# A transformer block in eight batches: two feed-forward moments taken between two score stages, and the tensor engine's order rewritten around them

## What is computed

```python
h = causal_conv1d(x, cond)                    # cond as taps, + bias
q, k, v = split(h @ qkv_w.T + qkv_b)          # 16 heads of 32
a = softmax(q k^T / sqrt(32) + alibi, causal) # first attention, 256 x 256 per head
x = x + (a v) @ out_w.T + out_b
Q, K, V = Wq, Wk, Wv applied along the tokens # second attention: 512 positions, 16 heads of 16
y = softmax((Q K^T / 4 + att_b) masked by cond) V
x = x + (silu(y @ gate_w.T) * (y @ up_w.T)) @ down_w.T
```

## Time and profile before

| what | value |
|---|---|
| three runs, without a profile | 1383.13, 1386.01 (median), 1388.77 us |
| profiled execution: its own time | 1393.41 us |
| profiled execution: span of the trace | 1391.6 us |
| PE busy in the span | 1223.9 us (88%) |
| DVE, ACT, POOL busy | 760.9 (55%), 522.3 (38%), 353.8 us (25%) |
| mean granted clock of PE in the span | 0.943 of full speed |
| one batch, second to seventh | 158.4 to 161.3 us |
| feed-forward of the last batch at the end | about 45 us |

### The profile page before, as it was taken

How to read it: one execution, slowest core, us unless ns; L and a number is a source line. 1 busy time by engine, 2 the same in 40 slices (tenths; PEclk the granted TensorE clock), 3 DMA queues, 4 the chain that set the end, 5 groups by cost and what they waited for, 6 DMA issues and landing times.

```text
span 1391.6 us, 21059 instructions
## 1 busy us (share of the span) xinstructions
PE 1223.9 (88%) x7528; PEld 683.2 (49%) x7528; DVE 760.9 (55%) x1173; ACT 522.3 (38%) x698; POOL 353.8 (25%) x202
## 2 busy tenths in 40 slices
PE   4485579899989999899998999889998999899988
PEld 3152235555445545546455555446455554455436
DVE  5344762557644674447724684447825585446732
ACT  1221145223533245323542246322552235332562
POOL 3075750065000920037000740027100550000000
PEclk9698579999999999999999999999999999999999
DMA  9866914255043722267042641257042650447124
GB/s 335 227 214 199 303 32 97 95 136 188 6 107 132 180 100 48 61 170 220 22 106 104 174 135 37 72 157 227 27 106 82 144 185 4 107 139 204 42 107 166
DMA packets 80481, 180.89 MB, mean 130 GB/s; under 512 B 14404, under 2 KB 54292, under 8 KB 70708
## 3 DMA queue, kind: packets, MB, share of 16 engines
q1 hardware_dynamic: 78352, 175.21, 43.2%
q0 software_dynamic: 1280, 4.20, 1.2%
q10 hardware_dynamic: 768, 0.26, 0.1%
HBM read 106.41 MB, written 21.14 MB: 92 GB/s over the span
## 4 chain that ended last, share of the span: by engine, by line
PE 66%; DVE 15%; DMA 6%; SPq 5%; issue 4%; ACT 2%; POOL 2%; DVEq 0%; ACTq 0%; POOLq 0%
PE psum L1076 9%; PE psum L1027 8%; PE psum L864 8%; PE psum L906 5%; DVE max L771 4%; PE psum L907 4%; PE psum L908 4%; PE psum L895 4%; PE psum L870 4%; SPq L392 4%; PE psum L1001 3%; PE psum L1063 3%; PE psum L884 3%; PE psum L992 2%; PE psum L959 2%
## 5 line engine op out<-in xcount | busy, mean ns | idle before, releaser
L771 DVE TENSOR_REDUCE max<-psum 128x1 f32<-128x512 f32 x512 | 325.9, 683 | 104.4 <-PE psum L1027 102.1
L630 ACT ACTIVATE probs<-psum 128x1024 f32<-128x1024 f32 x256 | 248.7, 1022 | 137.3 <-PE psum L1063 136.1
L1027 PE MATMUL psum<-k,q 52*128 52x512 f32 x512 | 181.4, 515 | 59.1 <-DMA k<-low 32.0
L518 POOL TENSOR_TENSOR h<-h_in,tap 128x1024 f32<-128x1024 f32 x7 | 13.3, 1898 | 645.3 <-DVE low L685 645.3
L1027 PEld LDWEIGHTS psum<-k,q 52*128 52x128 f32 x512 | 76.4, 199 | 194.2 <-DVE max L771 108.5
L1076 PE MATMUL psum<-probs,v 128*32 128x512 f32 x1024 | 142.0, 627 | 0.4 <-ACT probs L630 0.3
L864 PE MATMUL psum<-h,qkv_w 128*128 128x256 f32 x512 | 119.6, 388 | 18.2 <-DVE h L664 18.0
L591 ACT ACTIVATE probs<-psum 128x1024 f32<-128x1024 f32 x64 | 62.2, 1021 | 179.8 <-PE psum L978 179.8
L528 POOL TENSOR_TENSOR h<-h,products 128x1024 f32<-128x1024 f32 x49 | 123.0, 2511 | 3.8
L1063 PE MATMUL psum<-q,k 54*128 54x512 f32 x512 | 117.2, 452 | 7.2 <-DMA q<-max_l 5.8
L864 PEld LDWEIGHTS psum<-h,qkv_w 128*128 128x128 f32 x512 | 96.1, 192 | 48.4 <-issue 35.6
(11 more groups left out here) (103 smaller groups left out, 1641.2 us busy)
## 6 DMA issues: line engine op xcount, KB each, us to landing
stack<-wd_sorted SPq DMA_DIRECT2D x64, 1024.0 KB, 5.6
stack<-high SPq DMA_DIRECT2D x128, 128.0 KB, 2.4
stack<-low SPq DMA_DIRECT2D x64, 128.0 KB, 2.4
wd_sorted<-stack SPq DMA_DIRECT2D x8, 1024.0 KB, 5.1
q<-high SPq DMA_DIRECT2D x128, 64.0 KB, 5.0
k<-high SPq DMA_DIRECT2D x128, 64.0 KB, 3.1
h_in<-in_x_lanes SPq DMA_DIRECT2D x9, 512.0 KB, 3.9
x<-in_x_rows SPq DMA_DIRECT2D x8, 512.0 KB, 6.9
```

The lines of the kernel that those rows point to most:

```text
L630: nc.scalar.activation(probs[:, u // 2 % 2, u % 2 * 2:u % 2 * 2 + 2, :], psum[:, 2 + u % 2 * 2:4 + u % 2 * 2, :], ACT.Exp)\
L771: nc.vector.reduce_max(max2[:, g, e, i, t:t + 1], psum[:, SCORE_BANKS[s], :], AX_X).then_inc(S["s2_max"], 1)
L1027: nc.tensor.matmul(psum[:, SCORE_BANKS[s], :], r(q2[rows, g, i, t * P:(t + 1) * P]), r(k2[rows, g, i, :]), start=True, stop=True).then_inc ...
```

## The change

- `moments(0)` and `moments(1)` of the batch before are taken at the end of `scores1`, between the first and the transposed scores; later moments run two steps ahead of `gate_up`. ACT copies the first two right after it has issued the maxima's DMA. The transposed scores of the first two pairs wait for these copies, which read the banks that the scores write.
- In the window a step is now `gate_up(n)`, `moments(n + 2)`, two scores, the turn if any, half a `down`, two scores, the other half. In step 1 the half `down` comes ahead of the first two scores.
- Two of the four matmuls of `values(1)` are taken behind pairs 1 and 4 of `scores1`. The wait for the copied values moves from the first transposed score to the first product with them.
- The causal mask of `scores1` becomes two contiguous matmuls (256 and 128 columns) in place of one strided one (256).
- The low part of the first attention's maxima goes out on SP's queue, the high part on ACT's as soon as it is there.
- The split of the mask rows moves on DVE from the start of a batch to round 13 of the batch before.
- The output projection is ordered so that one matmul of the second token tile lies ahead of the last one of the first; the query and key projections have the contraction outside, and wait for each half of `x1` by itself.
- In a round two score tiles go ahead of the turn on PE, and two maxima ahead of it on DVE. Rounds 1, 5 and 6 use two banks, the others three; the first `turn_outputs` moves from round 5 to round 6. The first turn uses bank 2 instead of 5.

```diff
+
+AHEAD = 2
...
 TURN_AT = tuple(1 + (GS * (g + 1) - WINDOW_SCORES) // 4 for g in range(1, NG))
-OUT_AT = tuple(CT * (g + 1) + 1 for g in range(NG - 1))
+OUT_AT = tuple(CT * (g + 1) + (1 if CT * (g + 1) + 1 not in TURN_AT or g else 2) for g in range(NG - 1))
 
 SCORE_BANKS = [s % 2 for s in range(WINDOW_SCORES)]
 for _k in range(1, 1 + (NS - WINDOW_SCORES) // 4):
     for _s in range(4):
-        _free = (0, 1) if _k in TURN_AT and _k in OUT_AT else (0, 1, 7)
+        _free = (0, 1) if _k in TURN_AT or _k in OUT_AT else (7, 0, 1)
         SCORE_BANKS.append(min(_free, key=lambda x: len(SCORE_BANKS) - 1 - SCORE_BANKS[::-1].index(x)
                                if x in SCORE_BANKS else -1))
 LAST_IN_BANK = [max((r for r in range(s) if SCORE_BANKS[r] == SCORE_BANKS[s]), default=None) for s in range(NS)]
 V2_BANKS = (0, 1, 6, 7)
 Z_BANKS = (2, 5)
 GU_BANK, SUM_BANK = 3, 6
-TURN_BANKS = (Z_BANKS[1], 7, 7, 7)
+TURN_BANKS = (Z_BANKS[0], 7, 7, 7)
+
+PROJECTION = ((0, 0), (0, 1), (0, 2), (1, 0), (0, 3), (1, 1), (1, 2), (1, 3))
+
+VALUES_BEHIND = (1, 4)
 
...
 
                 if not first:
+                    wait("max1_low", 1)
+                    sp.dma_start(q1[MAX1 + 1:MAX1 + 2, :, :].rearrange("p h (t n) -> p (h t) n", t=LT), max1_l[:, :])\
+                        .then_inc(S["max1_rows"], 16)
...
                     nc.scalar.activation(z[:, n % 2, :], psum[:, Z_BANKS[n % 2], 0:L], ACT.Copy)\
                         .then_inc(S["z_out"], 1)
 
-                z_copy(0)
+                if ahead:
+                    for n in range(AHEAD):
+                        z_copy(n)
+                    return
                 taken()
                 for n in range(NT):
-                    if n + 1 < NT:
-                        z_copy(n + 1)
                     wait("gu_ready", n + 1)
                     if n >= 2:
                         wait("inter_low", n - 1)
                     nc.scalar.activation(inter[:, n % 2], psum[:, GU_BANK:GU_BANK + 2, 0:L], ACT.Silu)\
                         .then_inc(S["silu_out"], 1)
+                    if n + AHEAD < NT:
+                        z_copy(n + AHEAD)
                     wait("inter_out", n + 1)
                     if n >= 2:
                         wait("down_step", n - 1)
                 def wait(name, count):
                     act.wait_ge(S[name], at(b, name, count))
 
-                wait("max1_high", 1)
-                wait("max1_low", 1)
-                for i, part in enumerate((max1_h, max1_l)):
+                for i, (part, ready) in enumerate(((max1_h, "max1_high"), (max1_l, "max1_low"))[0:2 if first else 1]):
+                    wait(ready, 1)
                     act.dma_start(q1[MAX1 + i:MAX1 + i + 1, :, :].rearrange("p h (t n) -> p (h t) n", t=LT),
                                   part[:, :]).then_inc(S["max1_rows"], 16)
+                if not first:
+                    feed(b, ahead=True)
 
                 if first:
...
                         .then_inc(S["sum_out"], 1)
 
+            def mask_rows(b):
+                dve.wait_ge(S["aug_step"], at(b, "aug_step", 3))
+                nc.vector.tensor_copy(aug_h[:].bitcast(F32R), aug_f[:]).then_inc(S["aug_high"], 1)
+                dve.wait_ge(S["aug_high"], at(b, "aug_high", 1))
...
-                nc.vector.tensor_copy(aug_h[:].bitcast(F32R), aug_f[:]).then_inc(S["aug_high"], 1)
-                wait("aug_high", 1)
-                nc.vector.tensor_tensor(aug_f[:], aug_f[:], aug_h[:], ALU.subtract).then_inc(S["aug_low"], 1)
 
                 for n in range(0, H1, 2):
                     wait("s1_ready", n // 2 + 1)
                     totals(b)
 
                 for k in range(1, ROUNDS + 1):
+                    for s in round_scores(k, 0)[:2]:
+                        maximum(s)
                     if k in TURN_AT:
                         turn(TURN_AT.index(k) + 1)
-                    for s in round_scores(k, 0):
+                    for s in round_scores(k, 0)[2:]:
                         maximum(s)
+                    if k == VALUES_FROM and not last:
+                        mask_rows(b + 1)
                     for half in range(2):
                         if k == QK1_FROM + 2 * half + 2 and not last:
...
 
-            def moments(b, n, turned=True):
+            def moments(b, n):
                 if n >= 2:
                     pe.wait_ge(S["z_out"], fed(b, "z_out", n - 1))
-                if turned and n == TURN_STEP + 2:
-                    pe.wait_ge(S["max2_low"], at(b, "max2_low", 1))
                 for i in range(2):
                     for s in range(4):
...
                     for t in range(LT):
                         nc.tensor.matmul(bank[:, t * L:(t + 1) * L], r(q1[0:MAX1, i, t * P:(t + 1) * P]),
                                          r(k1[0:MAX1, i, :]), start=t == 0, stop=False, skip_group_check=True)
-                    last = nc.tensor.matmul(bank.rearrange("p (a n) -> p a n", n=P)[:, 0:LT * LT:3, :], ident_b[:],
-                                            mask_q[:, None, :].broadcast_to([P, 2, P]), start=False, stop=True,
+                    nc.tensor.matmul(bank[:, 0:L], ident_b[:], mask_q[:], start=False, stop=False,
+                                     skip_group_check=True)
+                    last = nc.tensor.matmul(bank[:, L + P:2 * L], ident_b[:], mask_q[:, 0:P], start=False, stop=True,
                                             skip_group_check=True)
                     if n % 2:
                         last.then_inc(S["s1_ready"], 1)
+                    if n % 2 and n // 2 in VALUES_BEHIND:
+                        values(1, (VALUES_BEHIND.index(n // 2),))
                 wait("s1_max", H1 // 2)
                 nc.tensor.transpose(psum[0:LT * H1, 7, 0:P], max1[:].rearrange("p h t -> p (h t)"), ident[:])\
                     .then_inc(S["max1_turned"], 1)
-
-                values(1)
+                values(1, range(len(VALUES_BEHIND), CT))
+                if feeds:
+                    wait("y_out", 0)
+                    for n in range(AHEAD):
+                        moments(b, n)
...
                 def values1(g):
                     wait("p1_out", 2 * g + 2)
+                    if g == 0:
+                        wait("v1_out", LT)
                     if g == 1:
                         wait("max1_low", 1)
                     elif g >= 2:
                                     start=kt == 0, stop=kt == LT - 1, skip_group_check=True)
                     last.then_inc(S["pv1_ready"], 1)
 
-                wait("v1_out", LT)
                 wait("max1_rows", 32)
                 for p in range(H1 // 2):
+                    if p < AHEAD and not first:
+                        pe.wait_ge(S["z_out"], fed(b, "z_out", p + 1))
                     if p >= 2:
                         wait("p1_out", p - 1)
...
-                for t in range(LT):
-                    for c in range(CT):
-                        if t == 0:
-                            wait("o1_out", c + 1)
-                        last = nc.tensor.matmul(psum[:, t, :], o1[:, c, t * P:(t + 1) * P], out_w[:, c, :],
-                                                start=c == 0, stop=c == CT - 1)
-                    last.then_inc(S["proj_ready"], 1)
-
-                wait("x1_out", LT)
+                for t, c in PROJECTION:
+                    if t == 0:
+                        wait("o1_out", c + 1)
+                    last = nc.tensor.matmul(psum[:, t, :], o1[:, c, t * P:(t + 1) * P], out_w[:, c, :],
+                                            start=c == 0, stop=c == CT - 1, skip_group_check=True)
+                    if c == CT - 1:
+                        last.then_inc(S["proj_ready"], 1)
+
                 wait("p1_out", H1 // 2)
                 for i, ready in ((0, "q2_ready"), (1, "k2_ready")):
-                    for o in range(LT):
-                        for t in range(LT):
+                    for t in range(LT):
+                        if i == 0:
+                            wait("x1_out", t + 1)
+                        for o in range(LT):
                             last = nc.tensor.matmul(psum[:, 2 + 2 * i + o, :], w2[:, i, t, o * P:(o + 1) * P],
-                                                    x1[:, t, :], start=t == 0, stop=t == LT - 1)
-                        last.then_inc(S[ready], 1)
+                                                    x1[:, t, :], start=t == 0, stop=t == LT - 1, skip_group_check=True)
+                            if t == LT - 1:
+                                last.then_inc(S[ready], 1)
...
                 def turn(g):
                     wait("s2_max", GH * CT * (g + 1))
                     if g == 0 and first:
-                        wait("k2_out", LT)
+                        wait("q2_out", LT)
                     elif g == 0:
-                        pe.wait_ge(S["z_out"], fed(b, "z_out", TURN_STEP + 1))
+                        pe.wait_ge(S["z_out"], fed(b, "z_out", NT - 1))
```

(23 more changed lines are left out.)

34 lines of the change are left out of this document (19 added, 15 removed).

## The result

The changed kernel takes **1369.07 us** (median of 4 runs, 1365.12 to 1379.27); the kernel before, beside it on the same chip, 1387.39 (4 runs). The ratio is 0.9885, 95% interval 0.985 to 0.9921: faster by 1.15%. I had forecast 1339, 47 us under the 1386 of the kernel before; the measured gain is 18 us, two fifths of that, and 1369 lies 5 us outside the range. The profiled execution took 1365.1 us, its span 1363.2 against 1391.6.

The account below looks back on a forecast made before the run. PE was taken to bound the kernel, with waits and clock falls behind them. Seven batches gave 26 us, eight sets of rounds 10, the end 0.3: -36.5; clock -10.5; 1386 became 1339, forecast range 1325 to 1349, wider range 1320 to 1364.

Parts of the forecast that it names:

- First scores: Start of a batch to the turned maxima: 0.6 + 0.4 us of added matmuls against 1.06 saved, no change.
- From the turn to the transposed scores: Between first and transposed scores: transposed scores start 0.55 us earlier, with 1.93 us of moments done for nothing.
- Projections: Output, query and key projections: matmuls fill PE's waits of 0.48 and 0.78 us, -1.26 us a batch.
- In front of the window: Value projection to the window's first score tile, and step 1: -3.6 + 0.55 + 1.1 = -1.95 us a batch.
- window: Window steps 2 to 8: same PE work, no new wait; -0 to +0.3 us a step, taken as 0.
- rounds: Score rounds 1, 5 and 6 with two banks: waits filled, -1.25 us a set, bounds +1.0 and -2.5.
- the chains bind where I have PE: Rival: values matmuls delay the turn, `rest(0)` takes longer, rounds gain nothing; 1367 us, range 1357 to 1379, chance 0.18.
- (2): Projections in the profile after: no PE waits of L992 on `o` and L1001 on `x`.
- (4): Rounds in the profile after: no wait for `max_l` in round 1; rounds 5 and 6 at 3.2 to 3.9 us each.
- (1): First scores: L940 within 1 us of now behind DVE's first maximum; first L974 about 4.0 us later, no wait over 0.3.
- (3): Window's front: no stack DMA wait, short `gate_up` wait for `gated`; step 1's second pair waits for maxima, 1.1 us together.
- (5): Whole steady batch in the profile after: 152 to 154 us, and 0.98 to 0.99 of the clock.

Follow-up runs that it names:

- the kernel with the moments behind the pairs: Changed kernel with the two moments behind pairs 1 and 4 of the first scores, all four values matmuls behind the turn: 1357.0 us, ratio 0.9788.
- the moments alone: Changed kernel with the new projection order and the new rounds undone, against the kernel before: 1395.91 us, ratio 1.0104.

## Why the prediction was wrong, step by step

The sign was right, and so was the clock: I had two thirds of the falls gone and 0.65 us of time for each us of full clock, and three quarters went, at 12.4 / 19 = 0.65. No run changes the clock alone, so this split between steps and clock rests on the stages. What failed is the sum of the steps, -36.5 us: of the 5.0 us that it has for a steady batch, the stages show 0.5 in the five batches behind a return of the loop and some 3 in the other two. By the prediction's own parts:

- *First scores*, "the turned maxima come at the same time as now": 0.6 later. PE's waits for maxima there fell from 1.80, 0.34 and 0.34 us to 0.26 and 0.17, so the fillers met a PE with little room left. The mask matmul stood at 0.07 us a head, "partly in its waits"; two contiguous ones take 0.47 - 0.36 = 0.11 us more a head than the strided one, and undoing them in the kernel with the moments behind the pairs gave 1.06 us. No run undoes the masks or the values matmuls in the changed kernel itself, so how the 0.6 divides between them is argued. 0.6 x 7 = 4 us.
- *From the turn to the transposed scores*, "start 0.55 earlier": 1.5 to 2.1 later, **the step that failed most**: 2.3 us off on average in five of seven batches, 11 us, and two of the four clock falls left come right behind that wait. The DMAs landed earlier than I said, 3.3 us behind the turn and not 4.0. I had taken for granted that nothing but data stands between the loop's last instruction and its first, and so put PE's own branch at nothing; it takes 3.3 to 3.8 us. In place of four of the eight large matmuls that hid it I put 32 small ones, and the sequencer reached the branch 2.4 us later; I named what the matmuls cost and not what lay under them. In the second and eighth batch, which no return precedes, the moments cost nothing and the scores do come early, 3.80 us behind the turn at full clock.
- *Projections*, -1.26: -1.80. The 0.54 more is not placed by a run; the matmuls behind the two waits, which were slow at first, fit. "SP's chain of stack DMAs with it" was wrong (alone, PE's wait for the stack grew by 0.65), but in the changed kernel nothing waits for that chain.
- *In front of the window*, -1.95, with *window* 0 and *rounds* -1.25: -1.1 measured for the three. The rounds gave -1.0 in the changed kernel (46.0 to 45.0) and -1.2 alone: right. So the other two gave 0.1 instead of 1.95. From the first `gate_up` to the first score tile it took 7.4 us (442.27 to 449.64) where I had 6.6, most of it the wait for `rest`, 0.99 instead of 0.44; and the 6.08 of the third batch that I compared with is 0.3 above what an undisturbed batch took before. The wait for the maxima was 0.78 and not 1.1. The window, "I take 0": four of the steps went from 5.9 to 6.1 us, inside "+0.3 a step", 0.8 in all, and `gate_up` behind two score tiles took 0.87 of that back in the stage up to the turn. That is 0.75 + 0.3 - 0.3 + 0.8, or 1.6 of the 1.85 that are missing.

For `rest(0)` the median row that I leaned on was the wrong one: it covers the last two of the eight feed-forwards, beside which GpSimd does nothing, and `rest(0)` itself, which in the kernel before took 0.69 in all six batches because of where it started. The Trainium skill's rule (SBUF — State Buffer, "Who interferes with whom"), which I charged at a quarter of its price, agrees with the trace: 2.43 us with GpSimd's work beside it, 0.72 with nearly all of that taken out.

Of the rivals, "the chains bind where I have PE" gave 1367, next to the result. Half of its reason was true (`rest(0)`, of whose 1.7 us more PE waits 0.99), the other half not: the turn came 0.6 later and not up to 1.9, and the rounds gained. Its price came out right by luck, through a cause that no rival had, the loop's return. What I had said would show the forecast wrong, a batch above 156 us, is what came; `rest` made PE wait 0.99, at the edge of my bound of 1; and the window took 42.7 us, where its 44.4 less the 3.6 moved ahead of it are 40.8.

Of what would show it, (2) and (4) came as written; (1) and (3) did not, as told above; of (5), the clock did and the batch didn't.

## What to carry to other kernels

Whatever long instructions stand at the end of a loop's body also hide the loop's return; here, with small ones in their place, 2.2 to 2.8 us of idle time whose releaser is "issue" appeared in every turn of the loop. Ask the profile for the loop's own line: the branch stands there with its duration. The VectorE instruction that got onto the critical path here takes 0.69 or 2.43 us by whether it starts ahead of a GpSimd instruction or 0.02 us behind it: price such a one at its place in the new order, not at its median over the kernel. Parts of a change needn't add: here they are worth +1.0%, -0.5% and -0.6% alone and -1.15% together. One part's waits seem to cost clock that another part's removal of waits gives back: the falls of the moments alone are gone once the projections are added.

## What I had not expected of the hardware

- PE's branch back to the top of the loop takes 3.3 to 3.8 us in every steady batch, 0.08 when it leaves the loop, and the next matmul starts 0.3 us behind it; under 3.6 us of matmuls already issued it is nearly free (0 to 0.44 us of idle time).
- Four large matmuls and 32 small ones with their weight loads make PE's sequencer reach the branch 2.5 us behind the turn; with eight large matmuls, which take nearly the same time (3.6 us against 3.9), it is 0.15 us.
- `rest` on DVE ends 0.55 us after the GpSimd instruction that runs when it starts (2.43 us in all), and takes 0.69 when it starts 0.16 us ahead of one, although that one works beside it.
- Two mask matmuls with contiguous output (256 and 128 columns) start the next instruction 0.47 - 0.36 = 0.11 us later than one of 256 columns whose output lies in two pieces.
- The clock fell to 0.72 and less over stretches of 4 to 6 us in which PE was busy 98 to 100%, in the window behind the projections' two waits (0.49 and 0.78 us), in five of six batches, and stayed at 1.00 over the same work in all six without these waits. What makes it fall there while PE is busy, and in other kernels here without these two waits, is open.
